# Layer one's convolution: one product for a pair of heads instead of two, columns picked by ScalarE, odd heads placed by transfers

## The reference, cut to what matters

```python
avg = jnp.cumsum(x, axis=1) / jnp.arange(1, l + 1)[None, :, None]
ci = avg.reshape(b, l, H, d)...                # H = 16 heads of d = 16 channels
pc = ci @ W_pe + b_pe                          # K = 31 taps for every token and head
energy = stt + jax.nn.sigmoid(gate) * dyn
w = jax.nn.softmax(energy, axis=-1)
for kk in range(K):
    out = out + w[:, :, kk:kk + 1] * padded[:, kk:kk + l, :]
v = conv_loc @ W_fc.T + residual               # then a layer norm
```

## Time and profile before

| stretch | us | PE busy | DVE busy | ACT busy | POOL busy |
|---|---|---|---|---|---|
| retention, first 1250 us | 1250.00 | 1176.15 | 1016.19 | 822.72 | 394.00 |
| mostly experts, 1250 to 1650 us | 400.00 | 399.44 | 225.69 | 237.56 | 254.91 |
| layer one, 2200 to 2400 us | 200.00 | 198.56 | 173.36 | 115.80 | 60.40 |

### The profile page before, as it was taken

One profiled execution on the slowest core, in us unless ns is written; L12 is line 12 of the kernel. 1 busy time (PEld: TensorE's weight loads), 2 busy tenths in 40 slices (PEclk: granted clock), 3 DMA queues, 4 the chain that ended last, 5 costly groups with the idle time before them and its releaser, 6 DMA issues.

```text
span 3478.2 us, 67597 instructions
## 1 busy us (share of the span) xinstructions
PE 3312.0 (95%) x25168; PEld 2784.9 (80%) x25168; DVE 2655.0 (76%) x6172; ACT 2077.6 (60%) x4055; POOL 1267.5 (36%) x1073
## 2 busy tenths in 40 slices
PE   7999999999996899999999469999999999999999
PEld 4888888888885789999999447888888888888888
DVE  5888888888877865555555488888888888888884
ACT  4677767776764556556655345555555555555554
POOL 1333333333331276666665333333233322323320
PEclk9999999999998999999999789999999999999999
DMA  5323332222212254444444365555655556555641
GB/s 179 101 85 104 109 112 82 89 81 80 73 34 92 67 124 93 107 107 105 95 106 94 69 136 106 126 128 125 127 127 119 124 125 129 129 124 127 129 102 41
DMA packets 746021, 366.38 MB, mean 105 GB/s; under 512 B 551278, under 2 KB 696246, under 8 KB 745558
## 3 DMA queue, kind: packets, MB, share of 16 engines
q1 hardware_dynamic: 717278, 319.57, 36.2%
q0 software_dynamic: 28416, 42.49, 6.6%
HBM read 224.93 MB, written 135.99 MB: 104 GB/s over the span
## 4 chain that ended last, share of the span: by engine, by line
PE 82%; DVE 8%; ACT 3%; issue 2%; DMA 2%; POOL 1%; SPq 1%; POOLq 0%; ACTq 0%; DVEq 0%
PE bank L2291 10%; PE bank L1609 10%; PE bank L1593 10%; PE bank L2305 10%; PE bank L850 9%; PE bank L830 9%; PE bank L2262 7%; PE bank L130 5%; PE bank L2241 3%; PE bank L2273 3%; PE bank L807 2%; DVE x L732 2%; DVE stats L643 1%; PE bank L2236 1%; ACT sides L1137 1%
## 5 line engine op out<-in xcount | busy, mean ns | idle before, releaser
L1489 DVE TENSOR_TENSOR hidden_low<-bank,hidden_high 128x512 fp32r<-128x512 f32 x256 | 176.2, 689 | 263.1 <-ACT hidden_high L1190 263.0
L1183 ACT ACTIVATE bank<-bank,fc_bias 128x512 f32<-128x512 f32 x256 | 169.5, 662 | 263.6 <-PE bank L1593 263.6
L850 PE MATMUL bank<-w_high,gT_low 128*128 128x256 f32 x1024 | 314.8, 307 | 1.8 <-DVE gT_low L722 1.8
L606 ACT ACTIVATE bank<-bank,b 128x512 f32<-128x512 f32 x256 | 168.7, 659 | 244.7 <-PE bank L830 241.9
L2049 ACT ACTIVATE bank<-bank,l_b 128x512 f32<-128x512 f32 x256 | 168.9, 660 | 237.1 <-PE bank L2291 236.9
L2305 PE MATMUL bank<-l_w_high,l_hidden_low 128*128 128x256 f32 x1024 | 307.6, 300 | 0.0
L2262 PE MATMUL bank<-bandT,window 128*32 128x96 f32 x5632 | 270.3, 344 | 24.7 <-DMA bandT<-bands 21.4
L850 PE MATMUL bank<-w_high,gT_high 128*128 128x256 f32 x1024 | 289.7, 283 | 0.0
L850 PE MATMUL bank<-w_low,gT_high 128*128 128x256 f32 x1024 | 289.6, 283 | 0.0
L2305 PE MATMUL bank<-l_w_low,l_hidden_high 128*128 128x256 f32 x1024 | 286.0, 279 | 0.0
L2305 PE MATMUL bank<-l_w_high,l_hidden_high 128*128 128x256 f32 x1024 | 285.5, 279 | 0.0
(11 more groups left out here) (372 smaller groups left out, 10752.1 us busy)
## 6 DMA issues: line engine op xcount, KB each, us to landing
bandT<-bands SPq DMA_DIRECT2D x352, 240.0 KB, 3.7
fc_full<-in_L_ffn_fc_wT SPq DMA_DIRECT2D x32, 1024.0 KB, 5.7
bands<-zeros SPq DMA_DIRECT2D x22, 768.0 KB, 7.5
x<-in_L_attn_x SPq DMA_DIRECT2D x32, 512.0 KB, 5.9
moe_output<-zeros SPq DMA_DIRECT2D x32, 512.0 KB, 6.2
x_after_retention<-x SPq DMA_DIRECT2D x32, 512.0 KB, 3.0
moe_input_and_gates<-xn SPq DMA_DIRECT2D x32, 512.0 KB, 4.6
moe<-moe_output SPq DMA_DIRECT2D x32, 512.0 KB, 7.3
```

What stands on the lines that cost most here:

```text
L850: m = pe.matmul(out, x, w, start=False, stop=f == KF - 1 and j == 2 and c % 2 == 1)
L1183: e.activation(bank[:, :], bank[:, :], ACT.Gelu, bias=t.b1[:, x, f:f + 1]).then_inc(s("hidden_full"), 1)
L1489: v.tensor_tensor(t.hidden.low[:, n % SLICES, :], K.banks[t.bank["expand", i, f, 0]][:, :], t.hidden.high[:, n % SLICES, :], ALU.subtract) ...
```

## The change

- `window` becomes [128, 8 pairs, 32]: both heads' 32 channels side by side, a plain copy of the bank. No zeros, and no wait for them.
- `convolve` has one product for a pair instead of two. The moving operand has both heads' columns, 192 of them (token by token: even head, odd head), against the 32 channels of both heads. Half of the results are of use: even channels in the even columns, odd channels in the odd ones.
- ScalarE makes two copies instead of one: every second column (odd) into a new tile `odd_heads` [128, 2, 96], two buffers, and every other second column (even) into `convT`, in all 128 partitions. In the partitions of odd heads that copy leaves the wrong values.
- A new step `place_odd` on SP overwrites those: four transfers of 16 partitions by 2 by 96 numbers (12 KB each) from `odd_heads` to `convT`, after ScalarE's two copies (`conv_taken`).
- `mix` waits for these transfers (`odd_placed0/1`, which reuse the semaphores `x_in0/1`) instead of ScalarE's copy.
- All numbers of `PLACES_D`, `STARTS_D` and `BANKS_D` are new.

```diff
@@ layer_one_tiles
-    t.window = K.ring(ctx, "window", 2, [P, H // 2, 2, 2 * t.HD])
+    t.window = K.ring(ctx, "window", 2, [P, H // 2, 2 * t.HD])
+    t.odd = K.ring(ctx, "odd_heads", 2, [P, KD, TT])
@@ layer_one_sync
+        elif name == "place_odd":
+            (i,) = args
+            n, size, place = b * NT + i, min(TT, K.S - i * TT), i * TT % t.CIRCLE
+            e.wait_ge(s("conv_taken"), n + 1)
+            for g in range(4):
+                rows = slice(32 * g + t.HD, 32 * (g + 1))
+                e.dma_start(t.convT[rows, :, place:place + size], t.odd[n % 2][rows, :, 0:size]).then_inc(K.later(f"odd_placed{n % 2}")[0], 16)
@@ layer_one_scalar, window_turn
-            e.copy(out, src).then_inc(s("window"), 1)
+            e.copy(t.window[n % 2][:, :, :].rearrange("p a d -> p (a d)"), K.banks[t.bank["window_turn", b, *args, 0]][:, 0:D]).then_inc(s("window"), 1)
@@ layer_one_scalar, convolve
+            if n >= 2:
+                e.wait_ge(*K.later(f"odd_placed{n % 2}", 4 * 16 * (n // 2)))
+            heads = K.banks[t.bank["convolve", b, i, 0]][:, 0:2 * KD * TT].rearrange("p (k t q) -> p k t q", k=KD, q=2)
+            e.copy(t.odd[n % 2][:, :, 0:size], heads[:, :, 0:size, 1])
             if before:
                 e.wait_ge(s("mixed"), before)
-            e.copy(t.convT[:, :, place:place + size],
-                   K.banks[t.bank["convolve", b, i, 0]][:, 0:KD * TT].rearrange("p (k t) -> p k t", k=KD)[:, :, 0:size]).then_inc(s("convT"), 1)
+            e.copy(t.convT[:, :, place:place + size], heads[:, :, 0:size, 0]).then_inc(s("conv_taken"), 1)
@@ layer_one_tensor, convolve
             for k in range(KD):
-                for odd in range(2):
-                    for g in range(4):
-                        pair = 4 * k + g
-                        m = pe.matmul(bank[32 * g:32 * (g + 1), k * TT:(k + 1) * TT], t.window[n % 2][:, pair, odd, :],
-                                      t.bandT[n % 2][:, :, g // 2 * H // 2 + k * t.HR + g % 2 * 2 + odd], start=odd == 0, stop=odd == 1)
+                for g in range(4):
+                    first = g // 2 * H // 2 + k * t.HR + g % 2 * 2
+                    out = bank[32 * g:32 * (g + 1), 2 * k * TT:2 * (k + 1) * TT].rearrange("p (t q) -> p t q", q=2)
+                    m = pe.matmul(out, t.window[n % 2][:, 4 * k + g, :], t.bandT[n % 2][:, :, first:first + 2], start=True, stop=True)
@@ layer_one_tensor, mix
-            pe.wait_ge(s("convT"), NT * b + -(-(ch + 1) * P // TT))
+            last = NT * b + -(-(ch + 1) * P // TT) - 1
+            for n in range(max(last - 1, 0), last + 1):
+                pe.wait_ge(*K.later(f"odd_placed{n % 2}", 4 * 16 * (n // 2 + 1)))
@@ PLACES_D (two lines of the table; the rest moves likewise)
+    "place_odd": (16.42, 17.41, 19.29, 20.63, 22.19, 23.48, 25.09, 26.73, 27.49, 29.36, 30.81),
-    "mix": (19.06, 20.4, 21.9, 24.8, 26.2, 27.7, 30.6, 31.43), "center_mid": (19, 20.4, 21.9, 24.8, 26.21, 27.7, 30.6, 32),
+    "mix": (19.18, 20.61, 22.1, 24.89, 26.55, 27.9, 31.18, 32.37),
```

More of the change, by code:

```diff
@@ L1630 @@
 PLACES_D = {
[L1631 to L1638, removed]
@@ L1639 @@
-    "mix": (19.06, 20.4, 21.9, 24.8, 26.2, 27.7, 30.6, 31.43), "center_mid": (19, 20.4, 21.9, 24.8, 26.21, 27.7, 30.6, 32),
-    "root_mid": (24.98, 32.56), "residual_mid": (25.83, 32.44), "stats_x3": (26.59, 34.51), "root_x3": (27.13, 35.02), "norm_x3": (27.48, 35.68),
-    "turn_mid": (29.71, 36.62), "load_out_row": 35.09, "gain_out": (42.68, 50.91), "result": (45.63, 54.65),
+    "l1_split": 0.61, "l1_low": 1.07, "l1_contract": 2.58, "share": (2.58, 10.19), "load": (0.28, 7.56),
+    "join": (4.39, 13.48), "add_in": (4.82, 12.83), "stats_in": (6.48, 14.21), "root_in": (8.4, 14.56),
@@ new lines @@
+    "norm_in": (8.77, 16.24), "load_bias_row": 4.78, "turn_in": (9.08, 17.2), "average": (9.59, 9.61, 18.03, 18.36),
+    "add_row": (11.64, 19.73), "kernel_product": (10.78, 12.79, 14.88, 16.78, 18.79, 20.83, 22.75, 24.72),
+    "gated": (10.69, 12.8, 14.84, 16.4, 18.65, 20.84, 22.64, 24.58),
+    "energies": (11.36, 13.53, 15.74, 17.78, 19.27, 21.61, 23.55, 25.44),
+    "exponentials": (11.59, 13.9, 15.82, 17.92, 19.86, 22.1, 24.0, 25.44),
+    "softmax": (12.32, 14.48, 16.37, 18.38, 20.51, 22.29, 24.24, 26.28),
@@ new lines @@
+    "load_band": (13.86, 15.88, 16.88, 18.65, 19.95, 21.42, 22.58, 24.27, 25.58, 27.03, 29.02), "load_gain_row": 16.91,
+    "window_turn": (15.96, 17.2, 19.03, 20.29, 21.74, 23.22, 24.78, 26.15, 27.32, 29.11, 30.46),
+    "convolve": (16.97, 18.07, 19.67, 21.03, 22.3, 23.95, 25.02, 26.9, 28.62, 29.73, 31.18),
+    "place_odd": (16.42, 17.41, 19.29, 20.63, 22.19, 23.48, 25.09, 26.73, 27.49, 29.36, 30.81),
+    "mix": (19.18, 20.61, 22.1, 24.89, 26.55, 27.9, 31.18, 32.37),
+    "center_mid": (19.26, 20.73, 22.08, 25.08, 26.53, 27.94, 31.27, 32.33), "root_mid": (25.46, 31.92),
@@ L2009, in layer_one_scalar @@
             n = b * NT + args[0]
-            if n == 0:
-                e.wait_ge(*K.setup("pool", "windows"))
             e.wait_ge(s("window_turned"), n + 1)
@@ L2014, in layer_one_scalar @@
                 e.wait_ge(s("conv_product"), n - 1)
-            all_of = t.window[n % 2][:, :, :, :]
-            out = bass.AP(all_of.tensor, all_of.offset, [all_of.ap[0], [4 * t.HD, H // 2], [3 * t.HD, 2], [1, t.HD]])
-            src = K.banks[t.bank["window_turn", b, *args, 0]][:, 0:D].rearrange("p (a e d) -> p a e d", e=2, d=t.HD)
-            e.copy(out, src).then_inc(s("window"), 1)
+            e.copy(t.window[n % 2][:, :, :].rearrange("p a d -> p (a d)"), K.banks[t.bank["window_turn", b, *args, 0]][:, 0:D]).then_inc(s("window"), 1)
         elif name == "convolve":
```

76 lines of the change are left out of this document (40 added, 36 removed).

## The result

The kernel after takes 3649.94 us (median of 4 runs, 3646.43 to 3654.81) against 3479.12, a ratio of 1.0494 with a 95% interval of 1.0482 to 1.0507. The forecast was 3435 us, its range ended at 3510: the kernel is slower by 171 us, and its time lies outside of the range. The profiled execution has a span of 3653.0 us and is read against the earlier trace rows.

The account below looks back on a forecast made before the run. TensorE was taken as the bound, busy 994.99 of 1000 us in layer one. The sum was 3478.2 - 117 (products) + 73 (wait at `mix`) = 3434, rounded to 3435 us, with a range of 3372 to 3510.

Parts of the forecast that it names:

- point 1: Convolution's products on TensorE: 8 instead of 16 a window, 0.81 us instead of 1.47, saving 117 us over 176 windows.
- point 2: ScalarE's one copy becomes two, some 3.5 us more a batch, hidden by itself: 0.
- point 3: 44 more issues a batch on SP's queue; what stands behind them has slack: cost 0, between 0 and 10 us.
- point 4: `mix` waits for copies, issues and landing, 5.0 us from a window's end; TensorE stands still 73 us in all.
- point 5: VectorE gets nothing added; 89% busy in a batch of 87.5 us, so no bound.
- The wait eats the gain: Rival at `mix` of chunks 1, 2 and 5: the way takes 5.8 us, stalls 142 us, 3503 us; chance 0.16.
- Nearly hidden: Rival at `mix`: issues overlap ScalarE's lag, landing stays near 1.7 us, stalls 21 us, 3382 us; chance 0.26.
- The round doesn't shrink: Rival at the convolution's products: paired columns cost 4 cycles each, nothing saved, 73 us of stalls, 3551 us; chance 0.09.

Follow-up runs that it names:

- e3: Kernel after without the four transfers, `mix` waiting for ScalarE's copies alone, and a product's two heads 8 apart instead of neighbours: 3502.22 us (one run).
- e7: Kernel after with every transfer still issued, but into other rows of its own source, and `mix` not waiting for it: 3454.09 us, ratio 0.9926.
- e1: Kernel after without `place_odd`'s transfers, `mix` waiting for ScalarE's copies alone: 3441.33 us, ratio 0.9885.
- e11: e5 with VectorE's tap sums, reciprocal and product by it left out, so weights aren't normalised: 3379.07 us, ratio 0.9706.
- e5: Kernel after without the transfers, in the order of the kernel before: 3455.87 us, ratio 0.9937.
- e4: Kernel after with the four transfers issued by ScalarE right after its second copy instead of by SP: 3737.32 us, ratio 1.0738.
- e8: Kernel after with ScalarE copies (odd heads over all rows, then four small even-head copies) replacing the transfers, in the old order: 3488.12 us, ratio 1.0030.
- e14: Kernel after with ScalarE copies replacing the transfers, new order, VectorE's product by the reciprocal sums moved to GpSimd: 3535.81 us, ratio 1.0160.

## Why the prediction was wrong

- *Products (point 1): right.* A window takes 0.82 us, forecast 0.81, and e3 shows the reason given for it: with heads far apart a window takes 1.50 us.
- *ScalarE (point 2): right* that the second copy is hidden; its 0.64 us are in the chain of the wait.
- *SP's queue (point 3): nearly right.* 0 to 10 us were allowed, e7 puts it at 13. What was wrong is to look only at what stands behind the new issues on SP. What stands ahead of them is the cost.
- *The wait at `mix` (point 4): the step that failed.* "I take 5.0 us, with 4.3 and 5.8 as ends", one value for all chunks. The free path is 4.3, but it holds only for windows for which SP is free; at the others it takes 6 to 10. The time that the order leaves between a window and its `mix` was forecast within 0.3 us; only the transfers' way was wrong, and where it was wrong is where TensorE waits:

| chunk | left, forecast | left, measured | transfers' way | waited in all |
|---|---|---|---|---|
| 0 | 4.4 | 4.6 | 6.6 | 34 |
| 1 | 3.8 | 3.7 | 4.4 | 16 |
| 2 | 4.0 | 4.1 | 4.4 | 17 |
| 3 | 4.4 | 4.7 | 6.1 | 33 |
| 4 | 5.5 | 5.4 | 9.5 | 63 |
| 5 | 3.8 | 3.7 | 4.5 | 18 |
| 6 | over 5.4 | 7.5 | 7.3 | 3 |
| 7 | over 5.4 | 5.7 | 8.1 | 44 |

Times are us. "Left" is the time from the end of a chunk's last window to where TensorE could have begun its `mix`, the way is from the same end to the last landing; both are medians of batches 2 to 14. In the case shown above it is `bands<-w`, 7.23 us behind the large transfers. The row that says so was there: the two writes at 4.21 us. The prediction set it aside with "these should mostly be issued by the time window 2 is done", and never looked at windows 0, 6 and 10, which in SP's order stand behind writes of weights (window 6 with a band load between), nor at window 5, which stands behind a band load that waits for such writes to land. The chunks were ranked by slack alone, so chunks 4 and 7 got 0 and had 63 and 44 us. The term was 73 us and measured 226 of waiting; without the wait the kernel is 196 us shorter (e7).
- *The clock.* No term stood for it. It fell to 0.95 in the stretch; products right behind a wait of 5.5 us took twice their time. It has no experiment of its own: it is within the 196 us. An estimate of its part: TensorE is busy for 86.6 us a batch (853.5 of 1000 at 101.48) where e7, with the same products, has 84.2 (950.92 of 1000 at 88.5), some 40 us in 16 batches.
- *VectorE (point 5): the second step that failed.* At 94% busy "its lateness would then begin to cost, a few us in all". Without any transfer 80 of the 117 us are missing (e1), and e11 gave 77 back. A busy share leaves out what an engine waits for inside its own chain: VectorE waits for GpSimd's addition to the energies, and that doesn't shrink with TensorE's list. The group in the kernel before and in e5:

```profile
L2136 DVE TENSOR_REDUCE top<-energies 128x16 f32<-128x496 f32 x128 | 85.5, 668 | 92.3 <-POOL energies L1959 92.1
```

```profile
L2131 DVE TENSOR_REDUCE top<-energies 128x16 f32<-128x496 f32 x128 | 85.5, 668 | 91.3 <-POOL energies L1959 91.2
```

- *The rivals.* "The wait eats the gain" named the mechanism, SP held by the writes of weights, but the wrong place (chunks 1, 2 and 5 have 50 of the 226 us), and 5.8 us where 8 to 10 were true at windows 6 and 10. "Nearly hidden" fell; even with no transfer at all its 3382 us aren't reached. "The round doesn't shrink" fell with the windows of 0.82 us.

The sum with what was measured: 3478 - 117 (products) + 80 (the gain that doesn't come, put down to VectorE's chain) + 13 (SP's load) + 196 (the wait, and its clock) = 3650 us. The three last terms are differences of runs (e1 against the sum's 3361, e7 against e1, the kernel after against e7), so the sum closes by its making; the 80 is what is left of the products' gain.

## What to carry to other kernels

A transfer on a path that TensorE waits for must be costed by what stands ahead of it in its queue at that place, window by window: one free value plus an allowance hides just the cases that decide. The order gives how much time there is, and it can be read off well; what the queue does at that place needs its own row. When a change shortens the bound, the next engine's own chain is the new bound, its waits counted in, and the busy share doesn't show it; leaving out a piece of that engine's work in both kernels does. And where a few partitions must move, four small copies in place can be dearer than they look: here they took as much as the gain, until another engine was relieved.

## What the runs showed of the hardware

- Two neighbouring float32 columns are read at the price of one: 16 records of 192 columns take 0.82 us in pairs and 1.50 us with the partners 32 bytes apart.
- A small transfer's issue held SP for 0.59 us at the median, but up to 3.56 us right behind the writes of weights; two such writes held it for 7.23 us behind large transfers. Issued by ScalarE, the transfers held ScalarE's arithmetic: 155.6 us of idle time ahead of one activation (e4).
- A ScalarE copy of 192 columns over 16 partitions is hardly cheaper than one over 128: in e8 311 ns against 321.
- GpSimd's addition to the energies took 1.26 us in the old order and 1.39 in the new, with the same operation and shape, and 1.29 in the new order once VectorE's product had moved to GpSimd (e14).
- TensorE's granted clock was 0.50 right behind a wait of 5.5 us, with the products at half their speed, and 1.00 again some microseconds of work later.
